# A two-layer attention and mixture-of-experts kernel: new step orders for four engines and new PSUM banks

## The reference

```python
x = x + L0_xattn(layernorm(x), ctx_768, Wq, Wk, Wv, Wo, bo)   # 8 heads of 64, context of 154 tokens x 96
x = x + L0_ffn(layernorm(x), ...)   # 16 experts of 64, top 4 from the best 2 of 4 groups, and a shared one of 128
x = x + L1_xattn(layernorm(x), ctx_768, Wq, Wk, Wv, Wo)       # 16 heads of 8
x = x + L1_ffn(layernorm(x), ...)   # 8 experts of 256, top 2 by logits with bias, and a shared one of 256
# each expert: (silu(x @ w1) * (x @ w3)) @ w2, summed with the router's weights
```

## Time and profile before

| what | value |
|---|---|
| device time, median of 3 runs | 231.79 us (231.2 to 233.03) |
| profiled execution, span | 230.0 us (no time of its own is given beside it) |
| instructions on PE, DVE, ACT, POOL | 1389, 480, 378, 127 |
| HBM read | 16.08 MB |
| granted TensorE clock | 1.00 in the windows read |

### The profile page before, as it was taken

One profiled execution on the slowest core, in us unless ns is written; L12 is line 12 of the kernel. 1 busy time (PEld: TensorE's weight loads), 2 busy tenths in 40 slices (PEclk: granted clock), 3 DMA queues, 4 the chain that ended last, 5 costly groups with the idle time before them and its releaser, 6 DMA issues.

```text
span 230.0 us, 4315 instructions
## 1 busy us (share of the span) xinstructions
PE 223.5 (97%) x1389; PEld 166.7 (72%) x1389; DVE 163.7 (71%) x480; ACT 155.3 (68%) x378; POOL 126.4 (55%) x127
## 2 busy tenths in 40 slices
PE   7999999999999999999999999999999999999994
PEld 3676765965889898889535563588878887888883
DVE  3589984788667863699948983564857775776874
ACT  2579999986679445672689778876365586745561
POOL 2765743899046937767492107209499400996540
PEclk9999999999999999999999999999999999999999
DMA  6890000000029925900600000028000003700002
GB/s 204 211 296 4 1 3 0 0 3 1 3 74 242 362 114 144 221 3 4 217 3 3 3 1 6 0 79 293 0 0 0 3 0 87 284 0 4 0 0 91
DMA packets 10172, 17.04 MB, mean 74 GB/s; under 512 B 3715, under 2 KB 5540, under 8 KB 9766
## 3 DMA queue, kind: packets, MB, share of 16 engines
q1 hardware_dynamic: 9926, 16.45, 23.5%
q10 hardware_dynamic: 224, 0.32, 0.4%
HBM read 16.08 MB, written 0.62 MB: 73 GB/s over the span
## 4 chain that ended last, share of the span: by engine, by line
PE 86%; ACT 6%; DVE 4%; POOL 2%; issue 1%; DVEq 0%; POOLq 0%
PE psum L1175 12%; PE psum L1179 11%; PE psum L1176 11%; PE psum L1348 7%; ACT prob L749 5%; PE psum L1410 5%; PE psum L1356 4%; PE psum L1358 3%; PE psum L1357 3%; PE psum L1466 3%; PE psum L1294 3%; PE psum L1306 3%; PE psum L1431 2%; PE psum L1270 2%; PE psum L1183 2%; PE psum L1454 2%
## 5 line engine op out<-in xcount | busy, mean ns | idle before, releaser
L703 POOL TENSOR_TENSOR act_s<-act_s,spread 128x512 f32<-128x512 f32 x35 | 44.3, 1293 | 20.2 <-DMA spread<-cw 14.5
L1175 PE MATMUL psum<-xT_hi,w_hi 128*128 128x512 f32 x108 | 43.9, 406 | 0.0
L1179 PE MATMUL psum<-xT_lo,w_hi 128*128 128x512 f32 x108 | 42.3, 392 | 0.0
L1176 PE MATMUL psum<-xT_hi,w_lo 128*128 128x512 f32 x108 | 42.2, 391 | 0.0
L798 ACT CAST q<-psum 128x512 fp32r<-128x512 f32 x35 | 20.4, 587 | 20.4 <-PE psum L1358 14.1
L1009 DVE TENSOR_TENSOR q<-psum,q 128x512 fp32r<-128x512 f32 x35 | 23.8, 687 | 13.5 <-ACT q L798 13.2
L788 ACT ACTIVATE act_s<-psum 128x512 f32<-128x512 f32 x39 | 23.0, 597 | 12.3 <-PE psum L1179 7.7
L1146 DVE TENSOR_REDUCE neg_max<-psum 128x2 f32<-128x308 f32 x64 | 26.2, 472 | 4.3 <-PE psum L1410 4.0
L703 POOL TENSOR_TENSOR hid<-hid,spread 128x512 f32<-128x512 f32 x13 | 16.6, 1296 | 18.9 <-DMA spread<-cw 14.6
L652 POOL TENSOR_TENSOR rstd<-vareps,minus_half 128x4 f32<-128x4 f32 x8 | 8.1, 1017 | 34.0 <-DVE vareps L910 34.0
L646 POOL TENSOR_TENSOR w_lo<-w_src,w_hi 128x768 fp32r<-128x768 f32 x12 | 21.7, 1830 | 8.3 <-ACT w_hi L718 8.3
(11 more groups left out here) (171 smaller groups left out, 469.6 us busy)
## 6 DMA issues: line engine op xcount, KB each, us to landing
spread<-cw SPq DMA_DIRECT2D x16, 256.0 KB, 4.9
spread<-cw SPq DMA_DIRECT2D x6, 512.0 KB, 5.7
w_src<-in_w SPq DMA_DIRECT2D x2, 1152.0 KB, 5.1
w_src<-in_w SPq DMA_DIRECT2D x1, 2304.0 KB, 11.6
spread<-cw SPq DMA_DIRECT2D x8, 128.0 KB, 3.0
w<-in_w SPq DMA_DIRECT2D x1, 576.0 KB, 6.6
out<-X SPq DMA_DIRECT2D x4, 128.0 KB, 1.8
wv<-in_wv SPq DMA_DIRECT2D x2, 192.0 KB, 4.7
```

The source lines that it names most:

```text
L703: pool.tensor_tensor(g, g, spread[:, slot, :], ALU.mult).then_inc(weighed, 1)
L1175: pe.matmul(dst, w_hi, xT_hi[:, b, :], start=True, stop=False)
L1176: pe.matmul(dst, w_lo, xT_hi[:, b, :], start=False, stop=False)
L1179: return pe.matmul(dst, w_hi, xT_lo[:, b, :], start=False, stop=True)
```

## The change

The program's strings for PE, ACT, DVE and POOL are replaced, with all of PE's bank numbers; PE's first nine steps (four kT, xT(0,0), vf, vf1, two q) and SP's string stay. Each kind's steps keep their order, so the set of instructions is the same. A helper `need` emits a wait only where the engine has not yet waited for as much on that semaphore. Waits that hung on a step being the first of its kind now stand at each step that needs them. `res` of sub-layer 1 no longer waits for its own result; `lnA` of sub-layer 2 does.

Some differences of order, read off the strings: a scores step more stands before pT(0,3,0); h1(1,0,0) stands ahead of pT(1,3,0), and xT(1,0) ahead of pT(1,2,1), pT(1,2,2) and vf1(1); on DVE all four route(1,1,·) come before the h3 product of tile 4 of batch 0; on POOL weigh(1,1,1) and place_k1s(3) come before lnA(2,0); xT(3,1) and gate(3,1) come after oT, onT and wo1 of batch 1 and 10.2 us more of FFN steps.

```diff
@@ -150,68 +150,68 @@
 PROGRAM = {
     "PE":
-        "kT.0 kT.1 kT.0 kT.2 xT.3 vf.1 vf1.4 q.2 q.3 q.4 xT.2 q.3 scores.4.0 scores.3.1 scores.2.5 scores.6.7 " +
-        "scores.0.4 vf.3 q.1 q.2 scores.3.5 scores.6.1 vs.7 pT.2 scores.7.0 pT.4 q.3 pT.2 q.5 pT.6 scores.1.4 " +
-        "pT.7 pT.5 pT.2 k1.6 pT.0 scores.1.7 pT.2 pT.0 pT.5 pT.2 scores.6.4 rest.2.0.1.3 scores.7.5 pv pv pv " +
-        "pv scores.7.0 scores.1.2 scores.3.4 pT.6 wo.5 pT.0 pT.6 wo.1 scores.0.5 pT.3 pT.2 k1.4 vf1.6 vs1.0 " +
-        "pT.5 pT.3 pT.1 pT.2 k1.7 xT.6 k1.2 pT.4 pT.1 pT.6 gate.3 rest.1.6.4.5 pv pv pv pv h1.4 h1.6 wo.5 " +
...
-        "wo.1 cwT.3 h1.4 h1.3 h3.1 h3.4 h1.7 h3.1 xT.3 h3.0 h1.6 h3.5 gate.3 h3.7 h3.2 down.4 down down h1.1 " +
-        "h1.6 h1.0 h3.1 h3.5 h3.0 down h1.6 down down down down cwT.3 h3.1 down h1.0 h3.3 h1.4 h1.0 h3.5 h1.4 " +
...
+        "kT.7 kT.6 kT.5 kT.4 xT.3 vf.6 vf1.4 q.5 q.3 xT.7 q.6 q.4 scores.1.2 scores.3.6 scores.5.4 vf.0 scores.7.1 " +
+        "q.2 q.0 scores.3.6 scores.5.2 q.0 scores.4.7 pT.1 pT.3 pT.0 q.6 scores.5.1 scores.3.2 pT.4 vs.6 pT.7 pT.5 " +
+        "k1.4 pT.1 pT.6 scores.3.7 scores.1.2 pT.4 pT.5 pT.6 pT.3 scores.0.4 rest.5.7.3.6 pv pv pv pv scores.2.0 " +
+        "scores.5.7 scores.1.4 wo.3 pT.0 pT.6 pT.5 wo.2 pT.7 scores.1.4 vs1.5 k1.2 pT.6 pT.3 pT.0 k1.7 xT.5 k1.4 pT.1 " +
+        "vf1.0 h1.2 pT.5 pT.1 pT.6 pT.3 gate.7 rest.1.5.3.6 pv pv pv pv wo.4 wo.6 cwT.7 h1.3 h1.5 h1.1 h3.6 h1.2 h1.0 " +
...
+        "vf1.0 h1.2 pT.5 pT.1 pT.6 pT.3 gate.7 rest.1.5.3.6 pv pv pv pv wo.4 wo.6 cwT.7 h1.3 h1.5 h1.1 h3.6 h1.2 h1.0 " +
+        "xT.7 h3.6 h1.5 h3.3 gate.4 down.7 h1.1 down h3.6 h3.2 down h1.5 h3.6 h1.1 h3.3 down h3.0 cwT.4 h3.2 down " +
...
     "ACT":
...
+        "kT split lnB kT kT kT xT lnB split xT q q score score score score score score score score score score score " +
+        "score score score score score score k1 score pT pT score pT score pT split place_k1 score pv score score pv " +
+        "score pv score pv score score score place_k1 score score place_k1 pT split score score lnB k1 k1 xT place_k1 " +
+        "place_k1 place_k1 place_k1 pT k1 place_k1 pT pT place_k1 split gate place_k1 pv pv split pv pv place_k1 cwT " +
+        "h1 lnB h1 h1 xT h1 gate h1 h1 h1 place_k1 h1 h1 h1 cwT split split h1 h1 h1 place_k1 lnB place_k1 h1 xT " +
+        "split h1 split h1 place_k1 qd split q1copy place_k1 h1 q1copy q1copy q1copy h1 mT split exp exp exp expR exp " +
+        "exp lnB expR xT exp split exp qd mT exp q1copy q1copy q1copy q1copy exp expR expR exp exp exp od exp exp exp " +
+        "mT exp od expR exp exp exp onT expR exp exp mT split exp exp exp expR lnB expR exp xT exp exp exp exp exp " +
...
     "DVE":
...
+        "pT pT k1 xT pT k1 pT pT k1 gate route route route route wo wo lnA vf1 h3 xT gate h3 route h3 route h3 route " +
+        "route h3 h3 h3 h3 h3 res lnA h3 h3 h3 xT h3 qd h3 h3 score1 score1 h3 score1 score1 score1 score1 score1 " +
+        "score1 score1 score1 score1 score1 score1 score1 h3 score1 score1 h3 score1 score1 score1 score1 score1 res " +
...
     "Pool":
-        "lnA split lnA bo bo split " + 7 * "norm " + "lnA norm place_k1s split split split lnA place_k1s " +
-        8 * "weigh " + "split split lnA " + 8 * "weigh " +
-        "split split lnA split place_k1s place_k1s split split split lnA split split weigh weigh weigh weigh " +
-        "weigh lnA " + 27 * "weigh ",
+        "lnA split lnA norm norm norm split norm split norm place_k1s bo norm norm lnA norm split place_k1s split bo " +
+        "lnA weigh weigh weigh weigh weigh split place_k1s weigh weigh weigh split weigh place_k1s lnA weigh weigh " +
+        "weigh weigh split weigh split split weigh weigh split lnA split lnA split weigh weigh weigh weigh weigh " +
+        "weigh weigh weigh split split weigh weigh weigh weigh weigh lnA weigh weigh weigh weigh weigh weigh weigh " +
+        "weigh weigh weigh weigh weigh weigh weigh weigh weigh weigh weigh weigh ",
@@ -434,10 +434,19 @@
         def bank(key):
             return psum[:, uses[key][0], :]
 
+        reached = {}
+
+        def need(eng, semaphore, n):
+
+            at = (id(eng), id(semaphore))
+            if n > reached.get(at, 0):
+                eng.wait_ge(semaphore, n)
+                reached[at] = n
+
         def wait_filled(eng, key):
 
             k, n, _ = uses[key]
-            eng.wait_ge(bank_ready[k], n)
+            need(eng, bank_ready[k], n)
 
         def reads_of(key):
 
@@ -451,7 +460,7 @@
 
         def wait_moved(eng, key):
 
-            eng.wait_ge(*reads_of(key))
+            need(eng, *reads_of(key))
 
         def wait_bank_free(eng, key):
 
@@ -814,8 +823,7 @@
                     g, j = step[1:]
                     if j == 0:
                         wait_moved(act, ("k1", g))
-                        if g == 0:
-                            act.wait_ge(loaded["const"], 16 * N_CONST)
+                        need(act, loaded["const"], 16 * N_CONST)
                     k = k_stack[:, g % 2, :].bitcast(F32).rearrange("p (b c) -> p b c", b=B)
                     act.mul(k1[:, :, g, j, :], k[:, :, 0:CTX], head_rows[:, j:j + 1]).then_inc(k1_placed, 1)
                 elif kind == "qd":
@@ -897,6 +905,8 @@
                     s, b = step[1:]
                     if (s, b) == (0, 1):
                         dve.wait_ge(loaded["x1"], 16)
+                    if s == 2:
+                        wait_moved(dve, ("y", 1, b))
                     settle()
                     for t in range(T) if s in (0, 2) else ():
                         if (s, b) == (0, 0) and t % 2 == 0:
@@ -1000,7 +1010,6 @@
                     xb = X[:, b * T:(b + 1) * T, :]
                     settle()
                     moved(dve.tensor_tensor(xb, bank(key).rearrange("p (t d) -> p t d", t=T), xb, ALU.add), key)
-                    wait_moved(dve, key)
                 elif kind == "hsplit":
                     n = hid_index[step[1:]]
                     m = n - first_split
@@ -1167,15 +1176,12 @@
 
         @block.tensor
         def _(pe):
-            def product3(dst, w_hi, w_lo, s, b, first):
-
-
-                if first:
-                    pe.wait_ge(xT_rounded, position[("xT", s, b)])
+            def product3(dst, w_hi, w_lo, s, b):
+
+                need(pe, xT_rounded, position[("xT", s, b)])
                 pe.matmul(dst, w_hi, xT_hi[:, b, :], start=True, stop=False)
                 pe.matmul(dst, w_lo, xT_hi[:, b, :], start=False, stop=False)
-                if first:
-                    wait_moved(pe, ("xT", s, b))
+                wait_moved(pe, ("xT", s, b))
                 return pe.matmul(dst, w_hi, xT_lo[:, b, :], start=False, stop=True)
 
             pe.wait_ge(idle_ready, 1)
@@ -1188,19 +1194,17 @@
                     wait_bank_free(pe, step)
                 if kind == "kT":
                     p = step[1]
-                    if p == 0:
-                        pe.wait_ge(loaded["ctx"], 16 * N_CTX)
+                    need(pe, loaded["ctx"], 16 * N_CTX)
                     filled(pe.matmul(bank(step)[:, 0:B * CP], wk0[:, p * P:(p + 1) * P],
                                      ctxT[0:CD, :, :].rearrange("k b c -> k (b c)"), start=True, stop=True), step)
                 elif kind in ("vf", "vf1", "vs", "vs1"):
 
+                    need(pe, loaded["ctx"], 16 * N_CTX)
                     if kind in ("vf", "vs"):
-                        if step == ("vf", 0):
-                            pe.wait_ge(loaded["ctxv"], 16)
+                        need(pe, loaded["ctxv"], 16)
                         w, k = wv0, CD
                     else:
-                        if step == ("vf1", 0):
-                            pe.wait_ge(loaded["kv1"], 16 * N_KV1)
+                        need(pe, loaded["kv1"], 16 * N_KV1)
                         w, k = wv1, CD + 1
                     if kind in ("vf", "vf1"):
                         if kind == "vf1":
@@ -1229,18 +1233,16 @@
                     filled(ins, step)
                 elif kind == "xT":
                     s, b = step[1:]
-                    if (s, b) == (0, 0):
-                        pe.wait_ge(loaded["ident"], 16)
+                    need(pe, loaded["ident"], 16)
                     for t in LN_ORDER:
                         pe.wait_ge(xn_ready[t // 2], 2 * (position[step] - 1) + t % 2 + 1)
                         ins = pe.transpose(bank(step)[:, t * P:(t + 1) * P], xn[:, b, t, :], ident[:, :])
                     filled(ins, step)
                 elif kind == "q":
                     b, p = step[1:]
-                    if (b, p) == (0, 0):
-                        pe.wait_ge(lo_of["wq0"], 1)
+                    need(pe, lo_of["wq0"], 1)
                     c = slice(p * P, (p + 1) * P)
-                    filled(product3(bank(step), wq_hi0[:, c], wq_lo0[:, c], 0, b, p == 0), step)
+                    filled(product3(bank(step), wq_hi0[:, c], wq_lo0[:, c], 0, b), step)
```

(16 more changed lines are left out.)

40 lines of the change are left out of this document (13 added, 27 removed), and 43 rows, old and new, of the table PROGRAM.

## The result

The changed kernel takes 233.09 us (median of 10 runs, 232.45 to 233.51), the kernel before 231.43 in the same comparison. The ratio is 1.0064, 95% interval 1.0048 to 1.008: slower by 0.64%, 1.5 us. The time lies inside the prediction's range (229.2 to 233.9) and inside the 1% that it calls "no change". But ten runs of each resolve less than 1%: the sign is clear, and the forecast of -0.2 had it wrong. The profiled run has a span of 231.2 (before 230.0) and took 233.02, so 1.8 us lie around the span, as assumed.

What follows compares the result with a forecast made beforehand. The prediction took PE (97% busy) as the bound, so an order wins only where PE waits. Its terms summed to -0.2 us from 231.8, giving 231.6 us, range 229.2 to 233.9.

Steps and rivals of the forecast that it cites:

- lnA of sub-layer 2: Batch 0's lnA on POOL, now behind weigh(1,1,1) and place_k1s(3), starts near 88.5: +0.2 us (0 to +3).
- Exps of batch 0: Before pT(0,3,0), one more scores step runs while PE waited for ACT's exps: -0.7 us (-0.7 to 0).
- LayerNorm of batch 1: Around xT(1,0), h1(1,0,0) fills PE's wait for the norm, but xn may come late: 0 (-0.7 to +0.7).
- xT(1,1) and gate(1,1): Two silus precede ACT's xT copy, and gate(1,1) has 0.68 us less PE work before it: +0.2 us (0 to 0.7).
- Router of batch 1: DVE routes before h3(1,0,4), so h3(1,0,8) on PE may wait for its bank: +0.5 us (0 to 1.5).
- DVE's stretch, expT pairs, scattered stalls: DVE at 109.7 to 117, -0.2 us; one more side-by-side expT pair, -0.3; short PE stalls in 117 to 150, -0.5.
- Router of sub-layer 3: Batch 0, gate to cwT: 4.15 us of PE work against about 4.7 needed: +0.5 us (0 to +1).
- Tail: Last stage: gate(3,1) to cwT(3,1) keeps 7.6 us of PE work, above 4.7; four more step-kind changes: +0.1 us (-0.1 to +1).
- 1: Rival: the stalls go and nothing new comes, so faster, 229.3 us; chance 0.20.
- 2: Rival: batch 1's spread lands late, weigh(1,1,1) holds lnA(2,0) on POOL; three us late gives 234.6 us; chance 0.10.
- 3: Rival: batch 1's late router in sub-layer 3 makes h3(3,1,6) and (3,1,7) wait on PE; 234.2 us; chance 0.06.
- 4: Rival: ACT's table switches around route(3,1) also cost a drain, delaying the cwT copy; 234 us; chance 0.02.

Runs made afterwards that it cites:

- i1: Order of the kernel before up to down(1,1,8), then the changed kernel's, banks renamed, place_k1s(2) and (3) earlier on POOL; ratio to before 0.9982 (0.9959 to 1.0005).

## Why the prediction was wrong, step by step

The size of three terms failed, and each for a wait or a queue that it left out: xT(1,1), lnA of sub-layer 2 and the tail. Together they took 2.08 us instead of 0.5. Term by term, each against the change of the table's last column:

- *Exps of batch 0, -0.7*: right, -0.60; pT(0,3,0) starts at 30.54 as said.
- *LayerNorm of batch 1, 0*: right, +0.12 (-0.48 cumulative at cwT(1,0)); the old gap of the earlier trace rows is gone and xT(1,0) loses 0.57 in its place. (By the prices above 0.9 us of work fewer stands ahead of xT(1,0), not 1.3.)
- *xT(1,1) and gate(1,1), +0.2*: **failed**, +0.84 (from -0.48 to +0.36). The term looked at ACT's copy of xT, and PE does not wait for that: gate(1,1) starts at 69.52, right behind the product ahead of it. What it left out is the wait for xn at xT(1,1) itself, +0.61 of the +0.84. A chain through DVE's route and lnA, POOL's rstd and shift and ACT's lnB sets that step, whatever PE has done. It had no margin before: lnB ended at 67.34 on ACT, and xT(1,1) started at 67.33. Now lnB ends at 67.02, only 0.3 earlier, while PE has 0.68 us of work less ahead of it and a lead of 0.48.
- *Router of batch 1, +0.5*: right, +0.56, at h3(1,0,8) as named, with the releaser named.
- *lnA of sub-layer 2, +0.2*: **failed**, +0.66. The place was right, the sum was not; rstd starts at 90.21 for 88.5. The term was built on 5.7 us from copy to weighing (it was 6.8, since the store took 3.09 us and not 1.83), on a copy that ends at 80.9 (it was 81.42, with two silus ahead of it on ACT), and on data ready at 88.1 (it was 89.6). The last has two parts: PE late by 0.9, and 0.44 us in which DVE's neg_mean stood (below). The term's bounds were 0 and +3, so the size was in the range; the value taken was near the optimistic end.
- Between xT(2,0) and down(1,1,8) I had no term: +0.22.
- *DVE's stretch, expT pairs, scattered stalls*, together -1.0: right in sign, too small: -1.44. By the same reckoning the stretch up to mT(0,1) gained 0.5 (for 0.2), the rest 0.9 (for 0.8). i1 shows that the gain is real.
- *Router of sub-layer 3, +0.5*: +0.33, near in size but by luck. +0.32 of it stands already at gate(3,0), ahead of the router. From there PE does wait 0.22 for cw at cwT(3,0), as the term has it, but the old order lost as much between these steps, in short pieces: +0.01.
- *Tail, +0.1*: **failed**, +0.58. I set PE's 7.6 us of work against 4.7 of the router without ACT's queue in it, and from gate(3,1) to the end of cw it was 8.1 (183.37 to 191.48). DVE was done with the first part of the route at 186.62; the exp ran at 190.26, behind hsplits that wait for DVE. The timeline of ACT:

```profile
187.39 0.59 ACT L807 CAST q<-psum 128x512 fp32r<-128x512 f32 x1 [0.23 <-DVE psum L1122]
...
188.36 0.60 ACT L807 CAST q<-psum 128x512 fp32r<-128x512 f32 x1
188.97 1.28 ACT L785 ACT_TABLE_LOAD   x1
190.26 0.23 ACT L785 ACTIVATE e_diff<-diff 128x32 f32<-128x32 f32 x1
```

PE lost 0.41 at cwT(3,1), where the old order lost 0.09. The rest is entries into products: a product step behind transposes or other narrow matmuls starts its second matmul some 0.32 after its first instead of 0.23. The timeline of PE behind cwT(3,1), and the next step, which follows a product:

```profile
191.54 0.28 PE L1328 MATMUL psum<-ident,cw 128*32 128x128 f32 x1 [0.25 <-DVE cw L1104]
191.58 0.48 PE L1182 MATMUL psum<-xT_hi,w_hi 128*128 128x512 f32 x1
191.89 0.40 PE L1183 MATMUL psum<-xT_hi,w_lo 128*128 128x512 f32 x1
...
192.36 0.40 PE L1182 MATMUL psum<-xT_hi,w_hi 128*128 128x512 f32 x1
192.60 0.39 PE L1183 MATMUL psum<-xT_hi,w_lo 128*128 128x512 f32 x1
```

PE takes about 0.1 us more for each such step. Behind cwT(3,0) the new order has 12 of them and the old one 8. I had priced four changes between kinds of step at 0.03 each. A change from one product to another costs nothing, and these cost three times that.

The misses, in the order of the list (the first two, +0.10 and +0.12, taken together), are +0.22, +0.64, +0.06, +0.46, +0.22, -0.44, -0.17 and +0.48, in sum +1.47: they lead from the -0.2 of the forecast to the +1.27 of the table. The forecast came as near as it did because a gain of 1.44 hides most of the losses. Of the rivals, 1 was wrong because of the gaps, 2 happened at a fifth of its size, 3 did not (no wait of PE for a product in the last stage), and 4 did not: the load starts 0.01 us behind the cast ahead of it and the activation again 0.01 us behind the load, so the drain that the Trainium skill adds ("ScalarE: Activation LUTs", "What ACT_TABLE_LOAD costs") is not on the path here either.

## What to carry to other kernels

Where a written order is changed, treat each result of another engine that PE needs as a gate: list what stands ahead of it in that engine's queue, DMA landings too, and where the old trace shows no margin, charge the whole work removed from in front of it. A gap removed ahead of such a gate is met again there; take work out of the queue that feeds the gate, or move it into that queue's idle time (0.76 us moved into idle time gained 0.56; the same step moved behind the consumer gained nothing). An order and its bank plan are judged together, and a stretch that really is faster shows the same length wherever it is entered (32.15 to 32.19 us in 17 kernels).
